# Gate weights spread by VectorE and DMAs in place of TensorE, in a graph layer with a gated expert network

## The reference: what is computed

```python
xn = layernorm(x)
agg = segment_sum(xn[dst_nodes], src_nodes); mean = agg / max(count, 1)
x = x + xn @ W1.T + b1 + mean @ W2.T + b2
xn = layernorm(x)
h = relu(relu(xn @ eW1[e] + eb1[e]) @ eW2[e] + eb2[e]); o[e] = h @ eW3[e] + eb3[e]
shared = relu(relu(xn @ sW1 + sb1) @ sW2 + sb2) @ sW3 + sb3
gates = softmax(xn @ gW + gb)
topv, topi = top_k(gates, 2); topw = softmax(topv)
x = x + shared + sum(o[topi] * topw)
```

## Time and profile before

| | us |
|---|---|
| median of 3 runs (lowest, highest) | 3190.23 (3190.14, 3193.08) |
| profiled execution: time | 3193.37 |
| profiled execution: span of the records | 3191.8 |
| PE busy, share of the span | 3083.1, 97% |
| DVE busy | 2671.9, 84% |
| ACT busy | 1942.1, 61% |
| POOL busy | 1842.0, 58% |

### The profile page before, as it was taken

The page is one execution under the profiler, slowest core; times in us unless marked ns, Lnnn a source line. Parts: engine busy times, 40 slices in busy tenths (PEclk is TensorE's granted clock), DMA queues, the critical chain, the costliest instruction groups (busy, mean ns, idle before and its releaser), DMA issues.

```text
span 3191.8 us, 61476 instructions
## 1 busy us (share of the span) xinstructions
PE 3083.1 (97%) x20817; PEld 2822.4 (88%) x20817; DVE 2671.9 (84%) x7211; ACT 1942.1 (61%) x3507; POOL 1842.0 (58%) x1554
## 2 busy tenths in 40 slices
PE   7999899999689999999999999999999999999998
PEld 7999899999678888889898989888888888888887
DVE  8988898885288888888888888888888888888886
ACT  5655565556455656565656566666666666666665
POOL 1788888888665555555555555555555555555540
PEclk9999999999899999999999999999999999999999
DMA  7777677777533333333333333333333333333320
GB/s 242 212 219 207 192 211 202 197 202 210 148 100 100 86 99 87 98 88 95 92 93 92 92 91 92 93 89 97 86 99 85 100 85 101 85 101 85 98 79 27
DMA packets 201824, 387.38 MB, mean 121 GB/s; under 512 B 106671, under 2 KB 109821, under 8 KB 201506
## 3 DMA queue, kind: packets, MB, share of 16 engines
q1 hardware_dynamic: 133906, 226.02, 26.0%
q10 hardware_dynamic: 30800, 102.42, 10.0%
q0 software_dynamic: 36800, 54.95, 7.4%
HBM read 236.11 MB, written 161.00 MB: 124 GB/s over the span
## 4 chain that ended last, share of the span: by engine, by line
PE 71%; POOL 1%; issue 0%; DVE 0%; ACT 0%; DMA 0%; POOLq 0%; DVEq 0%
PE acc L1127 25%; PE acc L1188 13%; PE acc L1097 13%; PE acc L1108 4%; PE acc L1110 4%; PE acc L1174 3%; PE acc L1151 3%; PE acc L1184 2%; PE acc L1143 1%; PE acc L1199 1%; PE acc L1137 1%; POOL rows L165 0%; DMA rows<-z_d,tab 0%; POOL e_oh L177 0%; ACT h2f L1232 0%
## 5 line engine op out<-in xcount | busy, mean ns | idle before, releaser
L165 POOL DMA_INDIRECT rows<-z_d,tab x500 | 580.2, 1160 | 612.7 <-DMA tab<-tab_d 478.7
L177 POOL TENSOR_SCALAR e_oh<-iota_sb,tab 128x250 fp32r<-128x250 f32 (+1 forms) x500 | 522.2, 1055 | 460.8 <-PE acc L1110 452.3
L1127 PE MATMUL acc<-x1T_hi,wl_hl 128*128 128x500 f32 x2400 | 665.4, 392 | 0.0
L386 POOL DMA_INDIRECT tab_d<-pair,idx x400 | 550.5, 1376 | 118.6 <-issue 112.0
L725 PE MATMUL acc<-w_hl,xT_hi 128*125 128x256 f32 x3200 | 575.1, 285 | 0.1
L1127 PEld LDWEIGHTS acc<-x1T_hi,wl_hl 128*128 128x128 f32 x2400 | 444.0, 188 | 84.0
L1188 PE MATMUL acc<-wl_hl,h_hi 128*125 128x256 f32 x2400 | 479.1, 282 | 0.0
L725 PEld LDWEIGHTS acc<-w_hl,xT_hi 128*125 128x125 f32 x3200 | 470.6, 190 | 0.0
L1389 DVE TENSOR_TENSOR h_lo<-h1f,h_hi 128x500 fp32r<-128x500 f32 x600 | 397.3, 676 | 48.9 <-ACT h_hi L1226 40.5
L1219 ACT ACTIVATE h1f<-acc,bl_sb 128x500 f32<-128x500 f32 x600 | 404.3, 674 | 14.4
L1188 PEld LDWEIGHTS acc<-wl_hl,h_hi 128*125 128x125 f32 x2400 | 391.8, 186 | 3.7
(11 more groups left out here) (144 smaller groups left out, 6384.5 us busy)
## 6 DMA issues: line engine op xcount, KB each, us to landing
xs<-in_x SPq DMA_DIRECT2D x100, 448.0 KB
z_d<-zs ACTq DMA_DIRECT2D x100, 448.0 KB
y_d<-ys ACTq DMA_DIRECT2D x100, 448.0 KB
y_sb<-y_d SPq DMA_DIRECT2D x100, 448.0 KB
x_sb<-in_x SPq DMA_DIRECT2D x100, 448.0 KB
out<-x_sb SPq DMA_DIRECT2D x100, 448.0 KB
codes_b<-code_d SPq DMA_DIRECT2D x25, 390.6 KB
rows<-z_d,tab POOLq DMA_INDIRECT x500
```

The lines of the kernel that those rows point to most:

```text
L165: pool.indirect_dma_start(out=rows[g.h][:, q, :], out_offset=None, in_=z_d, in_offset=bass.IndirectOffsetOnAxis(ap=tab[g.h][:, q, 0:1], ax ...
L177: pool.tensor_scalar(e_oh[:, q, w], iota_sb[:, w], tab[g.h][:, q, 1:2].bitcast(F32), None, ALU.is_equal).then_inc(S["e_oh_ready"], 1)
L386: pool.indirect_dma_start(out=tab_d, out_offset=bass.IndirectOffsetOnAxis(ap=idx[:, n:n + 1], axis=0), in_=pair[:, 2 * n:2 * n + ROW], in_ ...
L1127: mm = pe.matmul(bank[L1_BANKS[t]][:, 0:GN], wl1_hl[:, w, f, t * P:(t + 1) * P], (x1T_hi, x1T_lo)[a][:, f, :], start=n == 0, stop=n == 5)
```

## The change

DVE turns the weights. `wst` is now [128, 64]: the weights (16 columns, expert by group), their high parts and their low parts, then zeros. After the low parts are written, one DVE transpose turns each 32 x 32 block into `wst_T`. The new `spread_gates`, at the head of SP's step, waits for that, stores `wst_T` to `gate_d` in DRAM with four DMAs (32 partitions, pieces of 128 bytes), waits until all four have landed, and then issues six loads: four broadcasts of 500 weights to 64 partitions each (2000 bytes per partition, 128 KB each) into `gbc[0]` and `gbc[1]`, and two into the rows of `wT_r`. `gated` reads `gbc`, and waits for all four broadcasts; layer 3 waits for the two loads of `wT_r`. The four transposes, ACT's cast and the two selector products go, with the selector. The constants of the selector's input that split the third layer's biases stay as a small input `low`. PE's wait for `out_ready` of the block before, which protects banks 6 and 7, moves from the transposes to layer 3. The diff, cut to the second pass:

```diff
@@ -112,11 +111,15 @@
+        s_gst = sem("gates_stored")
+        s_gbc = sem("gates_spread")
+        s_gw = sem("gate_rows_loaded")
+        gate_f = gate_d.rearrange("c r p -> (c r p)")
-                 "gate_step gates_own exp_ready gates_ready wT_done wT_ready l1_done "
-                 "h1_relu_ready h1_hi_ready h1_lo_ready gate_bc_done l2_done h2_relu_ready "
+                 "gate_step gates_own exp_ready gates_turned l1_done "
+                 "h1_relu_ready h1_hi_ready h1_lo_ready l2_done h2_relu_ready "
...
@@ -1072,7 +1073,12 @@
             g1 = sb("g1", [SP_, NS], F32, c2)
             g2 = sb("g2", [SP_, NS], F32, c2)
             gpair = sb("gpair", [SP_, NS, NX, NX], F32, c2)
-            wst = sb("wst", [SP_, NS, NB3], F32, c2)
+            wst = sb("wst", [P, 2 * 32], F32, c2)
+            wst_T = sb("wst_T", [P, 2 * 32], F32, c2)
+            gbc = [sb(f"gbc{t}", [P, GN], F32, c2) for t in range(2)]
+            w_own = wst[0:SP_, 0:16]
+            w_hi = wst[0:SP_, 16:32]
+            w_lo = wst[0:SP_, 32:48]
 
@@ -1130,18 +1136,7 @@
                                                start=n == 0, stop=n == 5)
                                 n += 1
                         mm.then_inc(S["l1_done"], 1)
-                    pe.wait_ge(S["gates_ready"], i.n(1, 1))
-                    if i.c:
-                        pe.wait_ge(S["out_ready"], i.n(2))
-                    for s in range(NS):
-                        mm = pe.transpose(bank[6][0:NB3, s * SP_:(s + 1) * SP_], wst[:, s, :],
-                                          ident_sb[0:SP_, 0:SP_])
-                    mm.then_inc(S["wT_done"], 1)
                     layer2(0)
-                    pe.wait_ge(S["wT_ready"], i.n(1, 1))
-                    for t in range(2):
-                        pe.matmul(bank[6 + t][:, 0:GN], selg_r[:, t, :], wT_r[:],
-                                  start=True, stop=True).then_inc(S["gate_bc_done"], 1)
                     layer2(1)
                 if nxt:
                     pe.wait_ge(S["x1n_ready"], n1.n(NS, NS))
@@ -1180,6 +1175,9 @@
                         cols_ = slice(s * SP_, (s + 1) * SP_)
                         o = bank[6 + s // 2][0:SP_, (s % 2) * D:(s % 2 + 1) * D]
                         if s == 0:
+                            pe.wait_ge(s_gw, i.n(32, 32))
+                            if i.c:
+                                pe.wait_ge(S["out_ready"], i.n(2))
                             pe.wait_ge(S["h2_lo_ready"], i.n(H2T, H2T))
                         pe.matmul(o, wT_r[:, cols_], b3_r[:], start=True, stop=False)
                         n = 0
@@ -1250,9 +1248,6 @@
                     act.activation(gy[:], gd[:], ACT.Exp).then_inc(S["exp_ready"], 1)
                     for t in range(1, H1T):
                         h1_value(t)
-                        if t == H1T - 1:
-                            act.wait_ge(S["wT_done"], i.n(1, 1))
-                            act.copy(wT_r[0:NB3], bank[6][0:NB3, 0:GN]).then_inc(S["wT_ready"], 1)
                         h1_high(t)
                     h2_value(0)
                     h2_high(0)
@@ -1318,13 +1313,15 @@
                 gate_step(dve, i, 9, dve.tensor_reduce(g1[:], gd[:], AX.X, ALU.add))
                 gate_step(dve, i, 10, dve.reciprocal(g2[:], g1[:]))
                 if i.c:
-                    dve.wait_ge(S["wT_done"], i.n(1))
-                gate_step(dve, i, 11, dve.tensor_tensor(gd[:], gd[:], r4, ALU.mult))
-                gate_step(dve, i, 12, dve.tensor_copy(wst[:, :, 0:NX].bitcast(F32R), gd[:]))
-                dve.tensor_copy(wst[:, :, 2 * NX:3 * NX].bitcast(F32R), gd[:])\
-                   .then_inc(S["gates_own"], 1)
-                dve.tensor_tensor(wst[:, :, NX:2 * NX], gd[:], wst[:, :, 0:NX],
-                                  ALU.subtract).then_inc(S["gates_ready"], 1)
+                    dve.wait_ge(S["gates_turned"], i.n(1))
+                gate_step(dve, i, 11, dve.tensor_tensor(
+                    w_own.rearrange("p (e s) -> p s e", s=NS), gd[:], r4, ALU.mult))
+                gate_step(dve, i, 12, dve.tensor_copy(w_hi.bitcast(F32R), w_own))
+                gate_step(dve, i, 13, dve.tensor_tensor(w_lo.bitcast(F32R), w_own, w_hi,
+                                                        ALU.subtract))
+                if i.c:
+                    dve.wait_ge(s_gst, i.n(64))
+                dve.transpose(wst_T[:], wst[:]).then_inc(S["gates_turned"], 1)
 
             def edges_low(dve, g):
                 dve.wait_ge(S["e_hi_ready"], g.n(1, 1))
@@ -1391,9 +1388,9 @@
                                       ALU.subtract).then_inc(S["h1_lo_ready"], 1)
 
                 def gated(t):
-                    dve.wait_ge(S["gate_bc_done"], i.n(2, t + 1))
+                    dve.wait_ge(s_gbc, i.n(64, 64))
                     dve.wait_ge(S["h2_relu_ready"], i.n(H2T, t + 1))
-                    dve.tensor_tensor(h2f[t][:], h2f[t][:], bank[6 + t][:, 0:GN],
+                    dve.tensor_tensor(h2f[t][:], h2f[t][:], gbc[t][:],
                                       ALU.mult).then_inc(S["h2_gated"], 1)
 
                 def h2_low(t):
@@ -1465,7 +1462,36 @@
                   .then_inc(s_more, 16)
                 sp.dma_start(more_cnt[:], g.of(cnt_x)).then_inc(s_more, 16)
 
+            def spread_gates(sp, i):
+                wait_alone(sp, S["gates_turned"], i.n(1, 1))
+                if i.c:
+                    wait_alone(sp, s_gbc, i.n(64))
+                    wait_alone(sp, s_gw, i.n(32))
+                else:
+                    wait_alone(sp, S["cleared"], 6)
+                for b in range(4):
+                    n = min(32, SP_ - 32 * b)
+                    sp.dma_start(gate_d.rearrange("c r p -> r c p")[:, :, 32 * b:32 * b + n],
+                                 wst_T[32 * b:32 * b + 32, :].rearrange("r (c p) -> r c p", c=2)
+                                 [:, :, 0:n]).then_inc(s_gst, 16)
+                wait_alone(sp, s_gst, i.n(64, 64))
+                if i.c:
+                    wait_alone(sp, S["h2_gated"], i.n(2))
+                    wait_alone(sp, S["l3_done"], i.n(2))
+                for e in range(NX):
+                    sp.dma_start(gbc[e // 2][e % 2 * 64:e % 2 * 64 + 64, :],
+                                 gate_f[e * GN:(e + 1) * GN].partition_broadcast(64))\
+                      .then_inc(s_gbc, 16)
+                sp.dma_start(wT_r[0:2 * NX].bitcast(F32),
+                             gate_f[NX * GN:3 * NX * GN].rearrange("(k n) -> k n", n=GN))\
+                  .then_inc(s_gw, 16)
+                sp.dma_start(wT_r[2 * NX:3 * NX].bitcast(F32),
+                             gate_f[NX * GN:2 * NX * GN].rearrange("(k n) -> k n", n=GN))\
+                  .then_inc(s_gw, 16)
+
             def step_sync(sp, i, more):
+                if i.exists():
+                    spread_gates(sp, i)
                 if more and (i + 3).exists():
                     load_more(sp, i + 3)
                 if (i + 4).exists():
```

More of the change, by code:

```diff
@@ L63, in build @@
 def build(nc, x, src, dst, w1t, w2t, b12, wl1, bl1, wl2, bl2, wl3, b3, gw, gb,
-          ident, iota, codes, selg, tie, out, y_d, z_d, code_d, tab_d, tabx_d,
-          agg_x, cnt_x):
+          ident, iota, codes, low, tie, out, y_d, z_d, code_d, tab_d, tabx_d,
+          agg_x, cnt_x, gate_d):
     with ExitStack() as ctx:
@@ L87, in build @@
         b3_r = sb("b3_r", [P, D], F32R)
-        selg_r = sb("selg_r", [P, 2, P], F32R)
         rounds_sb = sb("rounds_sb", [1, 1], I32)
@@ L203, in build @@
                 st_b3b = sb("st_b3b", [NB3, D], F32, c0)
-                st_sel = sb("st_sel", [NB3, 3, P], F32, c0)
+                st_low = sb("st_low", [NB3, 2], F32, c0)
                 st_b = sb("st_b", [1, 2, D], F32, c0)
@@ L346, in _ @@
                                 sp.dma_start(st_b3[:], b3).then_inc(s_wl, 16)
-                                sp.dma_start(st_sel[:], selg).then_inc(s_wl, 16)
+                                sp.dma_start(st_low[:], low).then_inc(s_wl, 16)
                                 sp.dma_start(iota_sb[:], iota).then_inc(s_cst, 16)
@@ L535, in low_weights @@
                                 dve.wait_ge(s_small, 4)
-                                dve.tensor_scalar(st_b3b[:], b3_lo[:], st_sel[:, 2, 1:2], None,
+                                dve.tensor_scalar(st_b3b[:], b3_lo[:], st_low[:, 1:2], None,
                                                   ALU.mult).then_inc(s_small, 1)
                                 dve.memset(b3_r[:].bitcast(F32), 0.0).then_inc(s_small, 1)
-                                dve.memset(selg_r[:].bitcast(F32), 0.0).then_inc(s_small, 1)
-                                dve.wait_ge(s_small, 7)
+                                dve.wait_ge(s_small, 6)
                                 dve.scalar_tensor_tensor(out=b3_r[0:NB3], in0=b3_hi[:].bitcast(F32),
-                                                         scalar=st_sel[:, 2, 0:1], in1=st_b3b[:],
```

(22 more changed lines are left out.)

## The result

The changed kernel takes 3830.68 us (median of 4 runs, 3829.05 to 3839.53). The kernel before took 3191.65 beside it (4 runs, 3190.14 to 3193.49). The ratio is 1.2008, with an interval of 1.1993 to 1.2023. That is 639 us more, or 6.45 us for each of the 99 steps. The forecast was 3620 (4.35 a step), in a range of 3430 to 3900: the direction and the range held, the size was a third too small, and the time lies 111 us above the likeliest case's 3540 to 3720.

A forecast was written before the change was run, and what follows sets the result against it. PE was taken to bound the second pass, an unbroken run of matmuls. Per step, 2.9 us of lateness plus 1.45 for the clock made 4.35, over 99 steps 431 us, giving 3620 us; range over the cases 3430 to 3900.

The forecast's parts named there:

- the likeliest case: Whole kernel: PE stall plus clock loss in each step, 3620 us, range 3540 to 3720, chance 53%.
- Which engine, and where: Second pass, bound by PE: it waits for x1T_lo ahead of the edge sums' second half, 2.9 us late.
- The saving on PE: Four transposes and two selector products removed from PE: 0.89 us a step, 89 us in all.
- No cost of the load on the rest of the kernel, none on SP: Added transfers: SP is free for them, DMA engines idle from 1999 to 2002 us and 32% busy afterwards.
- First leg: Four stores to DRAM: three spacings of 0.43 us, a landing of 2.2 us, and 0.1 us before the broadcasts.
- Second leg: Four broadcasts back: three spacings of 0.43 us, then a landing of 2.45 us, 2.0 fixed and 0.45 for bytes.
- stall of 3.8 us: PE's wait for x1T_lo in each step: 2.9 us late plus the 0.89 us by which PE arrives earlier.
- The clock: PE's lowered clock after each stall: 1.45 us a step, bounds 0 and 3.4.
- The sum: Each step: 2.9 + 1.45 = 4.35 us, over 99 steps 431 us.
- Slow landings and the clock at every stall: Both DMA legs: landings of 3.3 and 3.75 us, 1.8 us for the clock, 7.1 us a step, 3895 us; 22%.
- The stall without the clock: PE in each step: 2.9 us late but clock kept at 1.00, 3480 us; chance 20%.
- The hidden round trip: DMA legs landing soon enough that PE does not wait and its saving is kept, 3101 us at best; 5%.

The follow-up runs named there:

- e1: Changed kernel with the spreading left out: no stores or broadcasts, weights of one from the start; 3127.81 us, ratio 0.9801.
- e2: Kernel before, plus DVE's transpose and all ten DMAs of a step, whose destinations nobody reads; 3194.39 us, ratio 1.0008.
- e10: Changed kernel with GpSimd's five gathers of a step held back until that step's broadcasts have landed; 3721.79 us, ratio 1.1664.
- e9: Changed kernel with each broadcast to 32 partitions in place of 64, so half the rows and bytes; 3646.66 us, ratio 1.1428.
- e6: Changed kernel with two of the four broadcasts issued by ACT, the other two by SP; 3819.01 us, ratio 1.1968.
- e4: Changed kernel with 20 unneeded matmuls on PE just ahead of its wait for x1T_lo in each step; 3668.87 us, ratio 1.1499.
- e5: Changed kernel with x1T_lo and other independent DVE and ACT work moved ahead of the gating products; 3340.02 us, ratio 1.0475.
- e8: Changed kernel with independent work before gating, broadcasts on SP and ACT, layer 3 starting with the ungated tile, DVE making gate weights first; 3150.31 us, ratio 0.9874.
- e12: e8 with all four broadcasts on SP and two of DVE's h1_low ahead of edges_low; 3151.69 us, ratio 0.9874.

## Why the prediction was right in direction and too small

- **Which engine, and where: right.** The kernel was bound by PE, with 0.6 us of slack behind the gating product. PE stands ahead of the second half of the edge sums, released by x1T_lo; nothing later took over. x1T_lo was complete 3.87 us after the product's start, where 3.86 was read from the earlier trace rows.
- **The saving on PE: too large.** 0.89 us a step forecast, 0.65 measured (e1).
- **No cost of the load on the rest of the kernel, none on SP: right.** e2 shows it with all ten DMAs in place. The other direction was put at nothing in the likeliest case and is not: the gathers add 0.9 us to the two legs (e10).
- **First leg: 3.6 forecast, 3.16 measured.** From the last store's start to the first broadcast's it is 1.8 us on average, not the 2.2 and 0.1 that I had taken from the lower end of the earlier trace rows.
- **Second leg: 3.75 forecast, 5.63 measured. This term of the sum was mis-sized.** I took the spacing of 0.43 us from the loads of y and x; it is 0.60 on average for these broadcasts (0.50, 0.64 and 0.64 in the step shown), 0.5 us over three of them. And the last landed 3.8 us after its start on average (3.5 in that step), not after 2.0 plus its bytes at 283 GB/s, 2.45; these 1.4 us are the larger part. Only the landing part was given a bound from the other side, the median of the earlier trace rows, and it was put with the rival; the spacing had none. e9 shows that both parts shrink when the rows and the bytes are halved, e10 that the gathers add 0.6, e6 that a second queue takes off 0.15. The two legs are 8.79 us together against 7.35, which is 1.4 of the error of 2.1. Added to the stall of 3.8 us that the prediction had, less the 0.24 of the smaller saving, they give 5.0; 4.9 was measured.
- **The clock: 1.45 forecast, about 1.95 measured (e4).** In the second pass each of PE's 97 stalls from 920 us on has a stretch at half clock that begins in it or just behind it. The rule of the Trainium skill that the prediction weighed (TensorE: Matmul & The Clock Gate, "HAM oscillation — how this bites in real kernels"), a wait for DMAs in each turn throttling every turn again, held here, in all 97. The rows of the first pass, in which two stalls of six cost nothing, were stalls of up to 3.4 us; this one is 4.9 us long. The mean over them was a poor guide for a longer stall: counted in the same way, 91 of 97 stalls have such a stretch in e9, where they are 3.5 us long on average, and 13 of 99 in e5, where they are 1.75.
- **The sum.** 4.91 us of stall over the whole pass, less 0.65, plus 1.95 is 6.2 of the 6.45 measured. The last 0.2 us stay open; they lie within the 2.3 that the half clock can have cost at most.
- **The rivals.** "Slow landings and the clock at every stall" (22%, 3895) was nearer to the truth than the forecast, 64 us off against 211: right about the clock at each stall and about slow broadcasts, wrong about slow stores. That the range held is owed to this rival, for whose sake it went up to 3900; the likeliest case alone would have missed. The stall without the clock did not occur. The hidden round trip did not occur either in this order of work, but e8 to e12 show that it can be had: not by shorter landings, as the rival had it, but by beginning the weights earlier and using them later.

## What to carry to other kernels

The detour through DRAM cost latency here, and no bandwidth that could be measured: count it as two landings and every issue between them, each with the times of a transfer of the same shape and direction, and put a bound on both sides of each. Before pricing it, list what stands behind the waiting instruction in its queue. Here moving 3.1 us of DVE's independent work ahead of the wait, with its part on ACT, recovered 491 of 639 us with the latency unchanged, and beginning the round trip earlier on top of a late use, with layer 3 beginning with the tile that needs no weights, turned a loss of 20% into a gain of 1.3%. And where the engine that bounds the kernel would get a stall in every turn, add the time it then runs at low clock; on this kernel that was 2 us for 5 us of stall.

## What was not expected of the hardware

- Issuing a broadcast took less time with half the rows and bytes. On SP's timeline four broadcasts to 64 partitions took 2.37 us, four to 32 partitions 1.72:

```profile
2515.66 2.37 SPq L1482 DMA_DIRECT2D gbc<-gate_d  x4
```

```profile
2116.04 1.72 SPq L1482 DMA_DIRECT2D gbc<-gate_d  x4
```

- Two broadcasts on ACT's queue took 1.36 us together in most steps of e6, begun in the same moment as two on SP, and 1.10 in e8, where they began 2.2 us after SP's first.
- Small stores to DRAM were quicker than the loads back: 1.7 us from the last start to the wait's end, against 3.5, in the step shown. The Trainium skill (DMA: Bandwidth & Descriptors, "Anatomy of one DMA") has about 2.0 us of fixed cost and a term for the bytes, for DMAs issued by GpSimd, which would give 2.3 us for a broadcast as an estimate; the median landing here was 3.4, and the measurement decides.
- The DVE transpose of 128x64 took 0.25 us, near the 0.22 forecast:

```profile
2512.36 0.25 DVE L1324 STREAM_TRANSPOSE wst_T<-wst 128x64 f32<-128x64 f32 x1
```
